# Which queue gathers the shorter low-row pieces of a banded 7x7 depthwise convolution

## The reference

```python
def _gn(v, G=32, eps=1e-5):
    B_, C_, H_, W_ = v.shape
    g = v.reshape(B_, G, C_ // G, H_, W_)
    m = jnp.mean(g, axis=(2, 3, 4), keepdims=True)
    s = jnp.var(g, axis=(2, 3, 4), keepdims=True)
    return ((g - m) / jnp.sqrt(s + eps)).reshape(v.shape)

x = x + conv3x3_depthwise(_gn(x), k, pad=1)
w_sym = (w + rot90(w, 1) + rot90(w, 2) + rot90(w, 3)) * 0.25
x = x + conv7x7_depthwise(_gn(x), w_sym, pad=3)
```

## Time and profile before

| | us |
|---|---|
| median of 3 runs | 3190.64 |
| lowest, highest | 3185.75, 3199.57 |
| the profiled execution, its own time | 3185.82 |
| its span | 3184.0 |
| PE busy | 2851.3 |
| DVE busy | 2818.7 |
| POOL busy (its DMA issues are counted) | 2188.2 |
| ACT busy | 2161.2 |

### The profile page before, as it was taken

One profiled execution on the slowest core, in us unless ns is written; L12 is line 12 of the kernel. 1 busy time (PEld: TensorE's weight loads), 2 busy tenths in 40 slices (PEclk: granted clock), 3 DMA queues, 4 the chain that ended last, 5 costly groups with the idle time before them and its releaser, 6 DMA issues.

```text
span 3184.0 us, 76492 instructions
## 1 busy us (share of the span) xinstructions
PE 2851.3 (90%) x28676; PEld 1805.6 (57%) x28676; DVE 2818.7 (89%) x5372; ACT 2161.2 (68%) x3969; POOL 2188.2 (69%) x2321
## 2 busy tenths in 40 slices
PE   0388999999999999999999999999999999999996
PEld 0155655565555655666665666655666665556663
DVE  3377999989999999999999999998999999999985
ACT  1175777777777776777777777776777776777771
POOL 3165767776777776777767677766777777777773
PEclk9898999999999999999999999999999999999997
DMA  3599888888888888888988888898888898888876
GB/s 89 139 237 232 234 233 232 233 228 224 229 234 232 240 236 216 238 231 232 243 223 237 227 239 236 231 241 223 226 230 244 231 237 227 232 237 227 241 174 174
DMA packets 966521, 712.45 MB, mean 224 GB/s; under 512 B 102918, under 2 KB 904710, under 8 KB 966086
## 3 DMA queue, kind: packets, MB, share of 16 engines
q1 hardware_dynamic: 511494, 383.52, 46.2%
q10 hardware_dynamic: 405504, 201.38, 22.3%
q0 software_dynamic: 49152, 122.65, 15.9%
HBM read 259.73 MB, written 220.81 MB: 151 GB/s over the span
## 4 chain that ended last, share of the span: by engine, by line
DVE 30%; POOL 22%; DMA 16%; issue 13%; PE 7%; ACT 6%; ACTq 3%; SPq 3%; DVEq 0%; POOLq 0%
POOL H L638 17%; DMA BT<-H 15%; DVE H L466 6%; DVE X L483 6%; DVE BT L506 5%; DVE BN L475 5%; PE PS L735 4%; PE PS L768 3%; POOL H L660 3%; ACTq L568 3%; ACT Z L557 2%; ACT H L554 2%; POOL BT L652 2%; SPq L268 2%; DVE TMP L429 1%
## 5 line engine op out<-in xcount | busy, mean ns | idle before, releaser
L735 PE MATMUL PS<-H,BAND 128*128 128x512 f16 x6912 | 1576.4, 388 | 79.4 <-DMA BAND<-rows 69.3
L735 PEld LDWEIGHTS PS<-H,BAND 128*128 128x128 f16 x6912 | 1019.6, 150 | 611.7 <-issue 100.1
L660 POOL TENSOR_TENSOR H<-Z,H 128x512 f16<-128x512 f32 x768 | 839.7, 1094 | 731.5 <-ACT Z L557 730.8
L768 PE MATMUL PS<-BT,BAND 118*32 118x512 f16 x21504 | 1258.2, 389 | 65.5 <-issue 37.2
L768 PEld LDWEIGHTS PS<-BT,BAND 118*32 118x32 f16 x21504 | 756.1, 132 | 521.8 <-issue 165.5
L554 ACT ACTIVATE H<-X,RB 128x512 f16<-128x512 f32 x768 | 619.4, 806 | 467.8 <-DVE H L466 439.2
L638 POOL TENSOR_SCALAR H<-X,RB 128x512 f16<-128x512 f32 x768 | 877.8, 1152 | 82.1 <-DVE RB L437 68.0
L506 DVE COPY BT<-BT 39x4256 f16<-39x4256 f16 x384 | 567.5, 1478 | 146.6 <-DMA BT<-H 136.8
L557 ACT ACTIVATE Z<-X,RB 128x512 f32<-128x512 f32 x768 | 615.5, 801 | 0.0
L537 ACT ACTIVATE Z<-X,RB 128x512 f32<-128x512 f32 x768 | 561.3, 802 | 30.4 <-issue 23.9
L580 ACT ACTIVATE DUMP<-X 128x512 bf16<-128x512 f32 x768 | 472.7, 617 | 149.2 <-DVE X L483 143.7
(11 more groups left out here) (48 smaller groups left out, 510.1 us busy)
## 6 DMA issues: line engine op xcount, KB each, us to landing
X<-in_x SPq DMA_DIRECT2D x768, 256.0 KB, 5.6
out_y<-X ACTq DMA_DIRECT2D x768, 256.0 KB, 6.6
BT<-H POOLq DMA_DIRECT2D x384, 162.1 KB, 5.2
BT<-H POOLq DMA_DIRECT2D x384, 149.6 KB, 5.2
BT<-H SPq DMA_DIRECT2D x576, 99.8 KB
BT<-H SPq DMA_DIRECT2D x384, 62.3 KB
BT<-H SPq DMA_DIRECT2D x192, 83.1 KB
rows<-v_all SPq DMA_DIRECT2D x8, 1638.0 KB, 11.2
```

Source lines behind the costliest of these rows:

```text
L660: g.tensor_tensor(part(H1, n, 1, img, O1, P1), Z[:, img, :].rearrange("p (c w) -> p c w", c=CC), part(H1, n, 0, img, O1, P1), ALU.subtract ...
L735: last = mm(PA[:, ch, :], band[:, j, ws, :], data[:, :, O1 - 1 + j:O1 - 1 + j + W], start=k == 0, stop=k == 3 * K1 - 1)
L768: last = mm(banks2(n)[b * BL:(b + 1) * BL, ch, :], band[:, j, :], rows, start=j == 0, stop=j == K2 - 1, tile_position=(0, b * BL))
```

## The change

SP's `gather_low` issues only the four longer pieces. A new function `gather_low_rest` on POOL issues the four shorter ones, between `gather_high` and `low_parts1`, after a wait for DVE's low rows of the same chunk. The pieces land on semaphores of their own, `low_rest_gathered`, for which `high_parts2` and conv 2 wait in addition. Sizes, places and data are the same.

```diff
-LOW_LANDED = 16 * NB * 2
+LOW_LANDED = 16 * NB
@@ semaphores
+        low_rest_gathered = [sem(f"low_rest_gathered{q}") for q in range(2)]
@@ sync, gather_low
-                    at1, at2 = LOW1 + r0, LOW2
+                    at1 = LOW1 + r0
                     middle = lo_row + SPLIT - r0
                     sp.dma_start(BT[at1:at1 + middle - lo_row, q, b, :, :],
                                  H2[lo_row:middle, q, 1, :, :]).then_inc(low_gathered[q], 16)
-                    sp.dma_start(BT[at2:at2 + hi_row - middle, q, b, :, :],
-                                 H2[middle:hi_row, q, 1, :, :]).then_inc(low_gathered[q], 16)
@@ gpsimd, high_parts2
                     wait_apart(pool, low_gathered[n % 2], ((at(n) - n % 2) // 2) * LOW_LANDED)
+                    pool.wait_ge(low_rest_gathered[n % 2], (n // 2) * LOW_LANDED)
@@ gpsimd
+            def gather_low_rest(n):
+
+                q = n % 2
+                pool.wait_ge(lo_done[1], NI * n + NI)
+                for b in (0, 2, 1, 3):
+                    lo_row, hi_row, r0 = window(b)
+                    middle = lo_row + SPLIT - r0
+                    pool.dma_start(BT[LOW2:LOW2 + hi_row - middle, q, b, :, :],
+                                   H2[middle:hi_row, q, 1, :, :]).then_inc(low_rest_gathered[q], 16)
@@ gpsimd, slot
                     gather_high(t - 4)
+                    gather_low_rest(t - 4)
@@ tensor, slot
                     pe.wait_ge(low_gathered[n % 2], ((at(n) - n % 2) // 2 + 1) * LOW_LANDED)
+                    pe.wait_ge(low_rest_gathered[n % 2], (n // 2 + 1) * LOW_LANDED)
```

## The result

The changed kernel takes 3380.61 us in the median (3376.6 to 3383.27), the kernel before, on the same chip, 3195.11 us (3185.75 to 3201.62). The ratio is 1.0582, with a 95% interval of 1.0549 to 1.0614. The prediction was 3194 us with a range up to 3265, so the change costs 185 us where next to nothing was forecast. In the profiled executions the span went from 3184.0 to 3381.5 us, 197.5 us more.

The account below looks back on a forecast made before the run. DVE's own work, 44.2 us a unit (three chunks), plus its gather wait sets the pace. 3185.82 plus 43 costs, minus 37 relief, minus 3 at the end gives 3189, as median 3194 us; own range 3165 to 3225, overall 3120 to 3265.

Parts of the forecast that it names:

- Second chunk, "+0.3 us for the copies, +0.1 us waiting": DVE beside 1.4 us of L660: copies +0.3 us, wait for conv 1 +0.1 us (bounds 0 and 0.5).
- rival 3: Second chunk's copies block L660 entirely, so DVE waits for conv 1; about 3250 to 3300 us, chance 0.06.
- Third chunk, "not late, with 0.1 us to spare": On POOL, L660 ends at 1644.0, scales come at 1644.1, so the high rows (L638) are not late.
- First chunk, "+0.3 us" (bounds 0 and 0.5): POOL's high rows (L638) now run into DVE's copy, which costs the copies 0.3 us.
- The sum: DVE's costs over the three chunks of a unit: 0.3 + 0.3 + 0.1 = 0.7 us, 43 us over 62 units.
- SP's relief, "0.6 us a unit": SP's earlier loads and long pieces shorten the copies' wait for the gather: 0.6 us a unit, 37 us in all.
- The issues, "0.5 us each, beginning when DVE's low rows end": POOL's four short issues a chunk, 0.5 us each, start at the end of DVE's low rows and meet no copy.
- The signs named: Profile marks for right or wrong, such as L506 busy +20 to 40 us, its gather wait 30 to 50 us down.
- The second chunk's last L660 at 1.5 us or more: Sign of being right, on POOL: that subtraction, slowed beside the copies, takes 1.5 us or more.
- Rival 2: POOL's delay is paid in full, without relief from SP: 3229 us, or 3260 if the third chunk's gather lands late; chance 0.22.

Follow-up runs that it names:

- e4: Changed kernel, but POOL issues the shorter pieces of only the third chunk of each unit and SP keeps the others; 3239.57 us, 1.0147 of the kernel before.
- e5: Changed kernel, but POOL issues the shorter pieces of only the first chunk of each unit and SP keeps the others; 3264.37 us, 1.0239 of the kernel before.
- e7: Kernel before, with all shorter pieces issued by ACT behind its squares instead of by SP; 3173.71 us, ratio 0.9945.
- e10: Changed kernel with L660 done for one of four channels; 3188.91 us, against 3168.74 us for the kernel before with the same thin L660.
- e8: Changed kernel with POOL's issues of the shorter pieces placed behind L660 instead of ahead of it; 3319.60 us, 1.0397 of the kernel before.
- e12: Kernel before, with the first and third chunks' shorter pieces issued by ACT, the second's kept on SP; 3171.71 us, ratio 0.9928.

## Why the prediction was wrong

*Second chunk, "+0.3 us for the copies, +0.1 us waiting": the step that failed first.* The prediction took from the earlier trace rows that the copies keep nearly their time and POOL gives way. Over the units, the pair of copies took 4.57 us in place of 3.03, +1.54 us. The row was misread in two ways. There the copy had begun first, at 3068.18 against 3068.20, and L660 waited; in the changed kernel L660 is running when the copy begins, and the copy waits. And the sum of the two copies hid that the second one waited as well. Asked for alone (DVE's timeline of the kernel before), it is

```profile
3069.47 2.05 DVE L506 COPY BT<-BT 39x4256 f16<-39x4256 f16 x1
```

where the first took 1.26 us: it lost 0.79 us to the L660 that ran at the time. The prediction's own numbers had L660 from 1625.4, the copy at 1628.38, and 1.4 us of L660 beside it. Read by who starts first, they give +0.3 us if the copy waits for the running L660 alone (the third, to 1628.67) and +1.4 us if it waits for the train; the runs show the train.

The Trainium skill (SBUF — State Buffer, Who interferes with whom) has the rule that the one to issue first keeps the shared ports for its whole instruction, and the other is blocked. The prediction named it only for rival 3, where the copies were to hold up L660; in the changed kernel the roles are the other way round. The traces agree with the direction. They go beyond it in one point: the copy waited 1.46 us, past the L660 that was running (to 1719.11) to the end of the next (1720.15).

*Third chunk, "not late, with 0.1 us to spare": failed.* L660 ends as reckoned, 6.5 us after DVE's low rows (1731.60 + 4.23 = 1735.83 against 1729.29, in the unit shown). But the scales are no fixed point. The product ahead of them has two inputs and waits for L660's end: over the units 1.55 us in place of 0.34, +1.2 us, all on DVE's path. e4 shows it alone. The 0.64 us at 1642.67 in the kernel before was the sign of it: that product was already held up once by L660, and the scales at 1644.1 already hung on it.

*First chunk, "+0.3 us" (bounds 0 and 0.5): right in what it counted.* The copies took 3.30 us in place of 2.87, +0.43. It left out the statistics that stand right before, MSQ and MQ. Over the units they took 1.53 + 0.69 = 2.22 us in place of 0.71: +1.5 us. The prediction searched for the copies only; no part of it asked which other DVE operations L660 would come to lie beside. e5 shows the two alone.

*The sum.* 0.43 + 1.54 + 1.2 + 1.5 = 4.7 us of DVE's time a unit, where 0.7 was taken. Busy time of DVE in a unit went from 43.52 to 48.12 us, 4.6. The period went from 46.61 to 49.86, +3.25 us, and 62 x 3.25 = 201 us, near the 197.5 of the span. The difference of 1.35 us is what the copies no longer wait.

*SP's relief, "0.6 us a unit": too small.* The wait for the gather fell by 72.8 us, 1.1 us a unit, where 30 to 50 us was forecast. The copies are also later now, which gives the gather more time, so this is not all relief. With the pieces on ACT it fell by 35.5 us (e7), inside the forecast, and the kernel gained 0.55%.

*The issues, "0.5 us each, beginning when DVE's low rows end": right.* 511 ns, and 1713.91 after low rows that end at 1713.61. That they cost DVE nothing themselves holds in e10 within 0.6%, together with the waits.

*The signs named.* L506's busy time went up by 117 us, not 20 to 40. SP's wait for DVE's low rows went up as said, from 290.5 to 913.3 us. Conv 1 of the third chunk began 2.0 us after the second chunk's copy (1720.72 against 1718.70), not 3.5. "The second chunk's last L660 at 1.5 us or more" did not come: the mean is 1089 ns. DVE waits for PE 14.8 us, not 50, so rival 3 as put is wrong, although its price, up to 3300, was nearest. Rival 2 had the right sign and a mechanism that did not occur: the copies wait less for the gather, not more. No rival had DVE's own instructions grow by more than the forecast did. Rival 2's 3229 us leaves out the offset that it names (3185.82 + 43 is 3228.8), which changes nothing here.

*Left open.* That DVE waits for more than one instruction is read from end times only, and the rows differ: the copy at 1718.70 and the product at 1734.47 waited past the end of one L660 for the next, while MQ at 1701.83 and, before, the copy at 3069.47 waited for one instruction. What decides between the two is not shown.

*PE's clock as a rival.* After the longer waits for MQ (247.0 us, 95.5 before), conv 1 is slower. PE's timeline after, and a window of it (us, busy us by engine, PEclk, DMA share, GB/s):

```profile
1702.61 0.39 PE L718 MATMUL PS<-MQ,ONES 128*128 128x8 f32 x2 [3.30 <-DVE MQ L495]
...
1705.00 9.28 PE L746 MATMUL PS<-H,BAND 128*128 128x512 f16 x36
...
1720.72 8.03 PE L746 MATMUL PS<-H,BAND 128*128 128x512 f16 x36
```

```profile
1705.00:1709.00 4.00, 4.00 (x17) 2.05 (x14) 3.42 (x13) 1.45 (x3) 2.88 (x5) 0.68 0.54 140
```

The granted clock was 0.68 at the start of the slower conv 1, behind idle time of PE, and its mean over the run fell from 0.974 to 0.944. But DVE does not pay for it: its waits for the results of both convolutions sum to 25.1 us after (14.8 + 10.3) and 24.2 us before (17.2 + 7.0). So the lower clock follows from DVE's lateness and is no cause of the 5.8% that these waits show.

## What to carry to other kernels

When an edit delays POOL, list everything on DVE that will then lie beside POOL's operations, down to the smallest two-input operation on the chain, and note, instruction by instruction, which of the two starts first: the one that starts first keeps its time. An operation paced by another engine leaves gaps; one that starts late, with all its input ready, runs as a train, and a short DVE operation behind it can cost as much as the rest of the train. Look for such a pair in the profile before, too: one L429 of 0.64 us among many of 0.16 us was there to be seen. If a queue has to be relieved, look first for an engine whose issues collide with nothing, here ACT (0.9945 and 0.9928), and compare with the bound from dropping the transfer (0.9727).

## What the runs showed of the hardware

- A DVE operation of 4 elements a partition with two inputs takes 0.16 to 0.17 us alone and up to 1.41 us beside a train of POOL's subtractions. Beside a train of L660 it ended within 0.2 us of the train's end in each row shown; beside four L638, MQ at 1701.83 waited for the first alone.
- POOL's four subtractions, begun before DVE's operation, keep their time: 4.23 or 4.24 us in every row shown, with DVE waiting beside them. Where the copy began first, one took 2.19 us in place of 1.09 (3068.20 in the kernel before).
- POOL's DMA issues beside a two-input DVE operation cost it nothing (MSQ 0.17 us in e8), while a DVE copy holds POOL's issues (1.94 us in e8, 3.87 us for four in the earlier trace rows). The Trainium skill (SBUF — State Buffer, Summary: rules for kernel authors) has the second of these, and the trace agrees.
- The other issuer saved only a little: 0.55 to 0.7% with ACT. The Trainium skill (DMA: Bandwidth & Descriptors, Issuing engines are not separate DMA queues) says that only issue time is saved, and the size of e7's and e12's gains is in keeping with it.
